# A fused Mamba and mixture-of-experts layer pair: shared-expert transposes between gate and up products, first expert tiles transposed early, two sets of spare rows

## The chip, the core and the metric

The kernel is one program on one core of a Trainium2 chip. The metric is the device time in microseconds (us), median of several executions. The engines are TensorE (PE, with its weight loads shown as PEld), VectorE (DVE), ScalarE (ACT), GpSimd (POOL) and SyncE (SP), which issues most DMAs. Each has its own in-order instruction stream; they meet by semaphores. TensorE writes into eight PSUM banks of 128 x 512 float32.

## The reference

Two residual blocks over x of 2 x 1024 tokens with 512 features, all in float32:

```python
x = x + attn(layernorm(x), ...)   # a Mamba block: in-projection, causal conv,
                                  # selective scan over 16 states, gate, out-projection
x = x + ffn(layernorm(x), ...)

def ffn(x):                       # T = 2048 tokens, H = 512
    h = rmsnorm(x) * norm_w ; flat = h.reshape(T, H)
    scores = softmax(flat @ router_w.T)            # E = 32 experts
    topk_w, topk_ids = top_k(scores, 4) ; topk_w /= topk_w.sum()
    routed = sum over the token's 4 experts of topk_w * (silu(g) * u) @ w2[e],
             with g, u = split(flat @ w1[e])       # 512 -> 2 x 256 -> 512
    shared = silu(flat @ sg) * (flat @ su) @ sd    # 512 -> 512 -> 512
    return x + routed + shared
```

Run on the given inputs, the reference's routing fills 79 tiles of 128 token slots, counted per expert and rounded up. The last expert has three of them.

## The kernel before

`front` (L109) holds everything up to the experts, `experts` (L1417 on) the routed part. Tokens stand in 16 tiles of 128.

**Mamba part.** Four segments of 512 tokens, 32 blocks `g` of (segment, 128 channels). It ends at about 1040 us. The change leaves its instructions alone, except on SP: after the first loads of the spread B and C rows, SP writes 128 zero rows behind `flat` (the normalised tokens in DRAM) and behind `out`, waits for both to land (`blank_stored`), and only then loads `w_out` and what follows in its queue.

**Shared part.** The order of TensorE's work is a written list, `closing_items()`. `ft(t)` transposes token tile t, `lg(t)` makes its router logits. Then, for each tile i, `gu(i)` is the gate product and the up product (8 matmul records each, of 128 x 512), into one pair of PSUM banks, `gu_ps[i % 2]`; `at(i)` transposes the activation (4 transposes), `dn(i)` is the down product (8 records), `rt(i)` the matmuls of the routing tables. The list runs `gu(i+1), at(i), dn(i), rt(i)`. ACT takes the silu of the gate (`silu_gate`, L775), copies the transposed activation from PSUM (`act_turned`, L780), and scales a residual row (`base_row`). DVE multiplies silu and up (`mult`, L957), adds the down product to the residual (`add`, L963), and between these computes the routing: `route_scores` ahead of `mult(0)`, `route_ids` behind it, `route_mask`, `route_counts`, `route_places`, `route_tables`, `route_hot` and `route_list` behind `add(0)` to `add(8)`. When the list of token slots is made, POOL gathers the rows of the first four expert tiles (`xg`, L1275). SP stores the finished residual rows to `out`.

**Expert part.** A barrier of all engines, then a loop over passes of four tiles, worked in pairs. `tiles` (L1445) skips passes that hold no tile, so 79 tiles make 20 passes and 80 tiles: the last one, tile 79, has only spare slots. For a pair TensorE makes `h` (L1613), transposes the rows of the next pair (`xT`, L1599), transposes the activation (L1624) and makes `y` (L1631). `rows_in` and `rows_out` for tiles 0 and 1 stand ahead of the loop. POOL gathers rows from `flat` (L1484) and scatters `y` into `out` with an add (L1499). Two tiles of one expert never hold the same token, so scatter j then need not wait for scatter j-1; otherwise `tile_wait[j]` makes it wait until that has landed. `same` in `route_counts` says which, and past the last expert it says "wait": every spare slot p of every tile points at the same row T + p.

## Time and profile before

| | us |
|---|---|
| median of 3 runs | 1807.21 |
| lowest, highest | 1803.53, 1816.69 |
| the profiled execution's own time | 1814.91 |
| its span, first to last instruction | 1813.2 |
| TensorE busy in the span | 1596.5 |
| mean granted TensorE clock | 0.963 of full |

The profiled execution lies 7.70 us above the median of the three. The Mamba part takes about 1040 us, where POOL and DVE are the fullest engines; the shared part runs from about 1075 to 1277 us, the expert part from there to the end, and in these two TensorE is the fullest.

### The profile page before, as it was taken

How to read it: one execution, taken by the hardware profiler on the slowest of the kernel's cores; microseconds unless marked ns; L12 is line 12 of the kernel's file. 1: busy time of each engine (PE TensorE's matmuls, PEld its weight loads, DVE VectorE, ACT ScalarE, POOL GpSimd, SP SyncE). 2: the span in 40 equal slices, each digit the busy share in tenths (PEclk: the TensorE clock that was granted, in tenths of full speed). 3: DMA queues.
4: the chain of work that ended last, by engine and by line, in shares of the span. 5: the costliest groups of instructions: out<-in, count | busy, mean ns of one | idle time of the engine just before them, and what ended most of it. 6: DMA issues, size and time to landing. Idle time of an engine off the chain costs nothing. (4 is left out here: it accounts for less than half of the span.)

```text
span 1813.2 us, 18146 instructions
## 1 busy us (share of the span) xinstructions
PE 1596.5 (88%) x4390; PEld 726.5 (40%) x4391; DVE 1187.3 (65%) x1675; ACT 736.4 (41%) x1231; POOL 1110.7 (61%) x704
## 2 busy tenths in 40 slices
PE   5678998899988999989887899999899999999995
PEld 2233433344433443333333364444444444444442
DVE  3599998999999989999999527531232323333331
ACT  4466566766566657666665421110011111111110
POOL 0199889998889998999999400010254454454442
PEclk9889998999999999999999999999999999999997
DMA  3620114101133111141000540010367686676653
GB/s 117 232 73 21 36 61 172 72 31 38 42 137 130 32 31 33 48 173 37 20 25 1 195 187 24 24 42 23 83 160 206 158 226 170 177 210 168 183 131 55
DMA packets 64838, 180.59 MB, mean 100 GB/s; under 512 B 10256, under 2 KB 15120, under 8 KB 56080
## 3 DMA queue, kind: packets, MB, share of 16 engines
q1 hardware_dynamic: 46704, 136.12, 21.3%
q0 software_dynamic: 18080, 43.82, 12.3%
q8 instruction: 25, 0.41, 0.1%
q14 instruction: 29, 0.24, 0.0%
HBM read 146.34 MB, written 33.57 MB: 99 GB/s over the span
## 5 line engine op out<-in xcount | busy, mean ns | idle before, releaser
L1217 POOL TENSOR_TENSOR h<-h,c_rep 128x2048 f32<-128x2048 f32 x128 | 579.4, 4530 | 34.7 <-DVE h L897 29.7
L1402 PE MATMUL bank<-h,ident 128*128 128x512 f32 x916 | 452.6, 638 | 95.6 <-POOL h L1217 74.7
L661 ACT ACTIVATE bank<-delta,a_neg 128x512 f32<-128x512 f32 x512 | 336.0, 682 | 183.2 <-DVE h L897 182.4
L1402 PEld LDWEIGHTS bank<-h,ident 128*128 128x128 f32 x916 | 181.1, 202 | 340.5 <-issue 211.9
L897 DVE TENSOR_TENSOR_SCAN h<-bank,state,h 128x512 f32<-128x512 f32 x256 | 305.9, 1260 | 0.2 <-ACT bank L661 0.2
L897 DVE TENSOR_TENSOR_SCAN h<-bank,h 128x512 f32<-128x512 f32 x256 | 290.7, 1200 | 2.0 <-ACT bank L661 2.0
L1613 PE MATMUL h_ps<-w_ring,xT 128*128 x640 | 284.8, 598 | 4.2 <-issue 4.2
L887 DVE TENSOR_TENSOR h<-bank,b_rep 128x2048 f32<-128x2048 f32 (+1 forms) x105 | 227.5, 2186 | 43.7 <-ACT bank L654 33.9
L1538 ACT ACTIVATE gs<-h_ps 128x256 f32<-128x256 f32 x80 | 30.7, 384 | 417.1 <-PE h_ps L1613 417.1
L1564 DVE TENSOR_TENSOR act<-gs,h_ps 128x256 f32<-128x256 f32 x80 | 33.7, 422 | 248.1 <-ACT gs L1538 248.1
L1613 PEld LDWEIGHTS h_ps<-w_ring,xT 128*128 128x128 f32 x640 | 120.7, 191 | 163.2 <-issue 163.2
L1631 PE MATMUL y_ps<-w_ring,aT 128*128 x320 | 148.7, 607 | 11.6 <-ACT aT L1542 11.5
L1483 POOL TENSOR_TENSOR held<-ones 128x1 f32<-128x1 f32 x78 | 22.2, 285 | 202.6 <-DVE which L1574 202.0
L1499 POOL DMA_INDIRECT out<-y,into x80 | 128.0, 1600 | 28.9 <-issue 26.4
L1204 POOL TENSOR_TENSOR h<-du,b_rep 128x2048 f32<-128x2048 f32 (+1 forms) x32 | 125.4, 3918 | 11.5 <-PE bank L1402 11.5
L1305 PE MATMUL bank<-xnT,w_in 128*128 128x512 f32 x256 | 118.5, 609 | 12.5 <-ACT zs L628 10.7
L1337 PE MATMUL bank<-xnT,w_res 128*128 128x512 f32 x256 | 120.3, 614 | 0.0
L1327 PE MATMUL bank<-w_out,xs 128*128 128x512 f32 x256 | 116.1, 597 | 0.0
L1484 POOL DMA_INDIRECT xg<-flat,which x78 | 79.3, 1016 | 22.6 <-POOL held L1483 12.0
L1498 POOL TENSOR_TENSOR sent<-ones 128x1 f32<-128x1 f32 x80 | 29.9, 373 | 97.7 <-DMA out<-y,into 85.8
L1631 PEld LDWEIGHTS y_ps<-w_ring,aT 128*128 128x128 f32 x320 | 57.8, 191 | 79.0 <-issue 79.0
L1274 POOL TENSOR_TENSOR held<-ones 128x1 f32<-128x1 f32 x4 | 0.8, 200 | 134.4 <-DVE which L1116 134.3
(213 smaller groups left out, 1746.4 us busy)
## 6 DMA issues: line engine op xcount, KB each, us to landing
w_ring<-in_w SPq DMA_DIRECT2D x32, 1024.0 KB, 6.0
b_rep<-bcd SPq DMA_DIRECT2D x16, 1024.0 KB, 6.8
c_rep<-bcd SPq DMA_DIRECT2D x16, 1024.0 KB, 4.8
w_ring<-in_w SPq DMA_DIRECT2D x32, 512.0 KB, 7.6
w_in<-in_w_in_x SPq DMA_DIRECT2D x32, 256.0 KB, 2.6
w_res<-in_w_in_res SPq DMA_DIRECT2D x32, 256.0 KB, 2.6
xa<-in_x SPq DMA_DIRECT2D x20, 256.0 KB, 3.0
xb<-in_x SPq DMA_DIRECT2D x16, 256.0 KB, 2.9
```

The costliest lines, as they stand in the source:

```text
L661: eng.activation(da[j][:], delta[:, g % 2], ACT.Exp, scale=a_neg[:, col:col + 1])\
L887: eng.tensor_tensor(h[:, q, a:b], du_ps[:].unsqueeze(1).to_broadcast([P, b - a, SEG]), b_rep[:, Q * q + a:Q * q + b, :], ALU.mult).then_in ...
L897: eng.tensor_tensor_scan(h[:, q, j, :], da[j][:], h[:, q, j, :], init, ALU.mult, ALU.add)\
L1204: eng.tensor_tensor(h[:, q, a:b], du[:].unsqueeze(1).to_broadcast([P, b - a, SEG]), b_rep[:, Q * q + a:Q * q + b, :], ALU.mult).then_inc(S ...
L1217: ins = eng.tensor_tensor(h[:, q], h[:, q], c_rep[:, Q * q:Q * q + Q, :], ALU.mult)
L1305: ins = eng.matmul(out[:], w_in[:, n % 2, k, :], xnT[:, s % 2, k, :], start=(k == 0), stop=(k == KC - 1))
L1327: eng.matmul(out[:], xs[:, s % 2, d, i * P:(i + 1) * P], w_out[:, d, :], start=(d == 0), stop=False)
L1337: ins = eng.matmul(out[:], w_res[:, i % 2, k, :], xnT[:, s % 2, k, :], start=(k == 0), stop=(k == KC - 1))
L1402: ins = eng.matmul(y_ps[:], c.ident[:], h[:, q, j, :], start=False, stop=(q == NQ - 1 and j == Q - 1))
L1499: eng.indirect_dma_start(out=dram.out_rows, out_offset=bass.IndirectOffsetOnAxis(ap=into[:, u:u + 1], axis=0), in_=y[:, u, :], in_offset=N ...
L1613: ins = eng.matmul(h_ps[i][:], xT[:, i, k, :], c.w1r[:, bass.ds(ring[i], 1), k, :].rearrange("p a n -> p (a n)"), start=(k == 0), stop=(k ...
L1631: ins = eng.matmul(y_ps[i][:], aT[:, i, k, :], c.w2r[:, bass.ds(ring[i], 1), k, :].rearrange("p a n -> p (a n)"), start=(k == 0), stop=(k ...
```

## The change

**Order.** `gu` is split into `gate` and `up`, with a semaphore each, and the list becomes `gate(i+1), at(i), up(i+1), dn(i), rt(i)`. `silu_gate` waits for the gate alone, `mult` for both.

**First expert tiles.** `xt(0)` and `xt(1)`, the transposes of the gathered rows of expert tiles 0 and 1, stand behind `at(15)` and ahead of `dn(15)`, into the banks of `gu_ps[0]`. DVE copies them to `xT` ahead of `add(15)`. `xT` now lies where `flat_T` of tiles 0 and 1 was. The expert part starts without them, its semaphores counted up to match.

**Spare rows.** A second set of 128 zero rows is written behind `flat` and `out`; spare slots of even tiles point at the first set, of odd tiles at the second (`trash`, from a fourth iota on POOL). `same` now is also 1 past the last expert. `wfull` goes; the weights are kept in `prob`. The list of slots is made with one instruction of another form (`miss`).

TensorE's order around shared tile 0, before (`w_sg` is the gate weight, `w_su` the up weight, `act_shared` the activation of tile i, `w_sd` the down weight; a wait stands in brackets):

```order
L1362 MATMUL bank<-w_sg,flat_T 128x512 [waits m_work_free0,f_shared_loaded]
L1362 MATMUL bank<-w_sg,flat_T 128x512 x3
L1362 MATMUL bank<-w_su,flat_T 128x512 x4
L1367 MATMUL bank<-ident,act_shared 128x128 [waits f_act_ready,m_work_free0]
L1367 MATMUL bank<-ident,act_shared 128x128 x3
L1372 MATMUL bank<-w_sd,act_shared_T 128x512 [waits m_work_free0,m_work_free1]
L1372 MATMUL bank<-w_sd,act_shared_T 128x512 x3
L1362 MATMUL bank<-w_sg,flat_T 128x512 [waits f_act_ready,m_work_free0,f_shared_loaded]
L1362 MATMUL bank<-w_sg,flat_T 128x512 x3
```

and in the change:

```order
L1372 MATMUL bank<-w_sg,flat_T 128x512 [waits m_work_free0,f_shared_loaded]
L1372 MATMUL bank<-w_sg,flat_T 128x512 x3
L1383 MATMUL bank<-ident,act_shared 128x128 [waits f_act_ready,m_work_free0]
L1383 MATMUL bank<-ident,act_shared 128x128 x3
L1372 MATMUL bank<-w_su,flat_T 128x512 [waits m_work_free0,f_shared_loaded]
L1372 MATMUL bank<-w_su,flat_T 128x512 x3
L1388 MATMUL bank<-w_sd,act_shared_T 128x512 [waits m_work_free0,m_work_free1]
L1388 MATMUL bank<-w_sd,act_shared_T 128x512 x3
L1372 MATMUL bank<-w_sg,flat_T 128x512 [waits f_act_ready,m_work_free0,f_shared_loaded]
L1372 MATMUL bank<-w_sg,flat_T 128x512 x3
```

The four transposes now stand between the gate and the up product, so that they are reached one product earlier, and the up product lies between them and the down product. On DVE nothing moves here: the `mult(0)` that gives `f_act_ready` still stands behind the whole of `route_scores`.

TensorE's order from shared tile 15's transposes into the expert part, before (`xg` are the gathered rows):

```order
L1367 MATMUL bank<-ident,act_shared 128x128 [waits f_act_ready,m_work_free0]
L1367 MATMUL bank<-ident,act_shared 128x128 x3
L1372 MATMUL bank<-w_sd,act_shared_T 128x512 [waits m_work_free0,m_work_free1]
L1372 MATMUL bank<-w_sd,act_shared_T 128x512 x3
L367 UNCONDITIONAL_BRANCH
L1589 UNCONDITIONAL_BRANCH [waits barrier_Pool_Activation_PE_DVE_SP_release]
L1599 MATMUL xT_ps<-ident,xg 128x128 [waits e_xT_ready,e_gathered0]
L1599 MATMUL xT_ps<-ident,xg 128x128 x3
L1599 MATMUL xT_ps<-ident,xg 128x128 [waits e_xT_ready,e_gathered1]
L1599 MATMUL xT_ps<-ident,xg 128x128 x3
L1447 UNCONDITIONAL_BRANCH
L1447 ISA
```

and in the change:

```order
L1383 MATMUL bank<-ident,act_shared 128x128 [waits f_act_ready,m_work_free0]
L1383 MATMUL bank<-ident,act_shared 128x128 x3
L1378 MATMUL bank<-ident,xg 128x128 [waits f_act_ready,e_gathered0]
L1378 MATMUL bank<-ident,xg 128x128 x3
L1378 MATMUL bank<-ident,xg 128x128 [waits f_act_ready,e_gathered1]
L1378 MATMUL bank<-ident,xg 128x128 x3
L1388 MATMUL bank<-w_sd,act_shared_T 128x512 [waits m_work_free0,m_work_free1]
L1388 MATMUL bank<-w_sd,act_shared_T 128x512 x3
L369 UNCONDITIONAL_BRANCH
L1603 UNCONDITIONAL_BRANCH [waits barrier_Pool_Activation_PE_DVE_SP_release]
L1463 UNCONDITIONAL_BRANCH
L1463 ISA
```

The eight transposes of `xg` moved from behind the barrier to ahead of the last down product. What follows the branch, the loads of the loop's registers and the first `h`, is unchanged.

The diff:

```diff
--- before.py
+++ after.py
@@ -160,4 +160,5 @@
         c.xg = over("xg", "xa", [P, PASS, ROW])
+        c.xT = over("xT", "b_rep", [P, 2, KC, P])
         c.which, c.held = new("which", [P, PASS], I32), new("held", [P, 1])
-        c.late = mem.home["b_rep"]
+        c.late = mem.home["b_rep"] + mem.size([P, 2, KC, P], F32)
         placed_at = [0]
@@ -183,4 +184,3 @@
         dest = inside("dest", [P, TT, TOPK])
-        wfull = inside("wfull", [P, TT, E])
-        trash, miss = inside("trash", [P, 1]), inside("miss", [P, NT])
+        trash_i, trash, miss = inside("trash_i", [P, NT], I32), inside("trash", [P, NT]), inside("miss", [P, NT])
         oh = inside("oh", [P, TOPK, TT, E])
@@ -233,5 +233,5 @@
         f_names = ("blank_made blank_stored shared_loaded stat mv_ready ln_chain rvar_ready ms_ready rrms_ready pool_chain "
-                   "scales_ready flat_ready base_made logits_done gu_done silu_done act_ready "
+                   "scales_ready flat_ready base_made logits_done gate_done up_done silu_done act_ready "
                    "iota_made chain max_ready exp_done mask_ready weights_ready counted tiles_ready tiles_turned hot_ready "
-                   "placed which_ready").split()
+                   "placed which_ready xt_done").split()
         F = {n: sem("f_" + n) for n in f_names}
@@ -314,3 +314,3 @@
         HALVED = ("out", "dtr", "bc")
-        UNBANKED = ("lg", "gu", "rt")
+        UNBANKED = ("lg", "gate", "up", "xt", "rt")
@@ -319,3 +319,4 @@
             last = lambda i, half: ("out", NSEG - 1, i, half)
-            ft, lg, gu = (lambda t: ("ft", 0, t, 0)), (lambda t: ("lg", 0, t, 0)), (lambda i: ("gu", 0, i, 0))
+            ft, lg, xt = (lambda t: ("ft", 0, t, 0)), (lambda t: ("lg", 0, t, 0)), (lambda u: ("xt", 0, u, 0))
+            gate, up = (lambda i: ("gate", 0, i, 0)), (lambda i: ("up", 0, i, 0))
             at, dn, rt = (lambda i: ("at", 0, i, 0)), (lambda i: ("dn", 0, i, 0)), (lambda i: ("rt", 0, i, 0))
@@ -326,5 +327,6 @@
             items += [lg(t) for t in range(8, 12)]
-            items += [gu(0), ft(12), ft(13), lg(12), ft(14), lg(13), ft(15), lg(14), lg(15)]
+            items += [gate(0), up(0), ft(12), ft(13), lg(12), ft(14), lg(13), ft(15), lg(14), lg(15)]
             for i in range(TT):
-                items += ([gu(i + 1)] if i + 1 < TT else []) + [at(i), dn(i), rt(i)]
+                items += [gate(i + 1), at(i), up(i + 1)] if i + 1 < TT else [at(i), xt(0), xt(1)]
+                items += [dn(i), rt(i)]
             return items
@@ -465,5 +467,6 @@
                 eng.wait_ge(F["blank_made"], 1)
-                eng.dma_start(dram.flat[T:T + P, :], blank[:]).then_inc(F["blank_stored"], 16)
-                eng.dma_start(dram.out[TT], blank[:, 0:DM]).then_inc(F["blank_stored"], 16)
-                eng.wait_ge(F["blank_stored"], 32)
+                for n in range(2):
+                    eng.dma_start(dram.flat[T + n * P:T + (n + 1) * P, :], blank[:]).then_inc(F["blank_stored"], 16)
+                    eng.dma_start(dram.out[TT + n], blank[:, 0:DM]).then_inc(F["blank_stored"], 16)
+                eng.wait_ge(F["blank_stored"], 64)
                 eng.dma_start(w_out[:], dram.w_out).then_inc(S["out_loaded"], 16)
@@ -557,3 +560,3 @@
                 eng.wait_ge(F["weights_ready"], 1)
-                eng.dma_start(dram.flat_w, wfull[:]).then_inc(c.weights_stored, 16)
+                eng.dma_start(dram.flat_w, prob[:]).then_inc(c.weights_stored, 16)
                 for i in range(3, TT):
@@ -775,3 +778,3 @@
                 def silu_gate(i):
-                    eng.wait_ge(F["gu_done"], i + 1)
+                    eng.wait_ge(F["gate_done"], i + 1)
                     after(eng, F["act_ready"], i - 1)
@@ -958,2 +961,3 @@
                     eng.wait_ge(F["silu_done"], i + 1)
+                    eng.wait_ge(F["up_done"], i + 1)
                     if i >= 2:
@@ -976,3 +980,3 @@
                     eng.tensor_tensor(prob[:], logits, row(mx[:], E), ALU.subtract).then_inc(F["max_ready"], 1)
-                    eng.wait_ge(F["iota_made"], 3)
+                    eng.wait_ge(F["iota_made"], 4)
                     for a, b in ((iota, iota_i), (iota_h, iota_i), (tok, tok_i), (thr, thr_i)):
@@ -1020,4 +1024,4 @@
                     ch.settle()
-                    eng.tensor_tensor(wfull[:], prob[:], mask[:], ALU.mult).then_inc(F["weights_ready"], 1)
-                    ch.add(eng.tensor_scalar(trash[:], tok[:, 0:1], float(T + 1), None, ALU.add))
+                    eng.tensor_tensor(prob[:], prob[:], mask[:], ALU.mult).then_inc(F["weights_ready"], 1)
+                    ch.add(eng.tensor_copy(trash[:], trash_i[:]))
                     ch.add(eng.tensor_scalar(tok1[:], tok[:], 1.0, None, ALU.add))
@@ -1040,3 +1044,3 @@
                     ch.add(eng.tensor_scalar(ecmp[:], end[:], tok[:, 0:1], None, ALU.is_lt))
-                    ch.add(eng.tensor_scalar(same[:], etile[:], float(E), None, ALU.is_lt))
+                    ch.add(eng.tensor_scalar(same[:], etile[:], float(E), None, ALU.is_ge))
                     ch.settle()
@@ -1046,3 +1050,3 @@
                     ch.settle()
-                    eng.tensor_tensor(same[:], same[:], eprev[:], ALU.mult).then_inc(F["tiles_ready"], 1)
+                    eng.tensor_tensor(same[:], same[:], eprev[:], ALU.max).then_inc(F["tiles_ready"], 1)
                     eng.tensor_scalar(etile[:], etile[:], float(E - 1), None, ALU.min).then_inc(F["tiles_ready"], 1)
@@ -1110,3 +1114,3 @@
                     slots = count_ps[:, LISTED:LISTED + NT]
-                    ch.add(eng.tensor_scalar(miss[:], slots, 0.0, trash[:], ALU.is_equal, ALU.mult))
+                    ch.add(eng.scalar_tensor_tensor(miss[:], slots, 0.0, trash[:], ALU.is_equal, ALU.mult))
                     ch.settle()
@@ -1155,2 +1159,7 @@
                         mult(i + 1)
+                    if i == TT - 1:
+                        for u in (0, 1):
+                            eng.wait_ge(F["xt_done"], u + 1)
+                            eng.tensor_tensor(c.xT[:, u], gu_ps[0][u][:].rearrange("p (k t) -> p k t", k=KC),
+                                              c.norm_f[:].unsqueeze(2).to_broadcast([P, KC, P]), ALU.mult)
                     add(i)
@@ -1264,2 +1273,3 @@
                 eng.iota(thr_i[:], pattern=[[P, NM]], base=0, channel_multiplier=0).then_inc(F["iota_made"], 1)
+                eng.iota(trash_i[:], pattern=[[0, NT // 2], [P, 2]], base=T + 1, channel_multiplier=1).then_inc(F["iota_made"], 1)
@@ -1355,3 +1365,3 @@
                             ins.then_inc(F["logits_done"], 1)
-                    elif kind == "gu":
+                    elif kind in ("gate", "up"):
                         eng.wait_ge(F["shared_loaded"], 16 * len(shared))
@@ -1359,6 +1369,12 @@
                         after(eng, F["act_ready"], i - 1)
-                        for w, to in ((w_g, gu_ps[i % 2][0]), (w_u, gu_ps[i % 2][1])):
-                            for k in range(KC):
-                                ins = eng.matmul(to[:], flT[:, i, k, :], w[:, k, :], start=(k == 0), stop=(k == KC - 1))
-                        ins.then_inc(F["gu_done"], 1)
+                        w, to, made = {"gate": (w_g, gu_ps[i % 2][0], "gate_done"), "up": (w_u, gu_ps[i % 2][1], "up_done")}[kind]
+                        for k in range(KC):
+                            ins = eng.matmul(to[:], flT[:, i, k, :], w[:, k, :], start=(k == 0), stop=(k == KC - 1))
+                        ins.then_inc(F[made], 1)
+                    elif kind == "xt":
+                        eng.wait_ge(c.gathered[i], 16)
+                        eng.wait_ge(F["act_ready"], TT - 1)
+                        for k in range(KC):
+                            ins = eng.transpose(gu_ps[0][i][:, k * P:(k + 1) * P], c.xg[:, i, k * P:(k + 1) * P], c.ident[:])
+                        ins.then_inc(F["xt_done"], 1)
                     elif kind == "at":
@@ -1431,3 +1447,3 @@
         sent = sb("sent", [P, 1])
-        xT = sb("xT", [P, 2, KC, P])
+        xT = c.xT
         gs = sb("gs", [P, 2, FI])
@@ -1549,3 +1565,3 @@
                 eng.sem_inc(S["y_ready"], 2)
-                eng.sem_inc(S["xT_ready"], 2)
+                eng.sem_inc(S["xT_ready"], 2 + 2)
                 eng.sem_inc(S["which_ready"], U)
@@ -1584,4 +1600,2 @@
-                for i in (0, 1):
-                    rows_out(i, i)
                 tiles(eng, pair)
@@ -1590,3 +1604,3 @@
             def _(eng):
-                eng.sem_inc(S["xT_done"], U)
+                eng.sem_inc(S["xT_done"], U + 2)
                 eng.sem_inc(S["aT_done"], 2)
@@ -1634,4 +1648,2 @@
-                for i in (0, 1):
-                    rows_in(i, 0, i, 0)
                 tiles(eng, pair)
@@ -1675,6 +1687,6 @@
     d.bcd = nc.dram_tensor("bcd", (NB * HALVES, 2 * NS, SEG), F32, kind="Internal").ap()
-    d.out = nc.dram_tensor("out", (TT + 1, P, DM), F32, kind="ExternalOutput").ap()
+    d.out = nc.dram_tensor("out", (TT + 2, P, DM), F32, kind="ExternalOutput").ap()
     d.out_rows = d.out.rearrange("t p n -> (t p) n")
     d.x1 = nc.dram_tensor("x1", (TT, P, DM), F32, kind="Internal").ap()
-    d.flat = nc.dram_tensor("flat", (T + P, ROW), F32, kind="Internal").ap()
+    d.flat = nc.dram_tensor("flat", (T + 2 * P, ROW), F32, kind="Internal").ap()
     d.flat_seg = d.flat[0:T, 0:DM].rearrange("(s t p) n -> s p t n", t=ST, p=P)
```

## Rows read from the trace of the kernel before

**Rows 1.** The page: the span.

```profile
span 1813.2 us, 18146 instructions
```

**Rows 2.** Stretches (from:to, length, busy by engine, clock, DMA share, GB/s), most of the shared part.

```profile
1100.00:1270.00 170.00, 158.39 (x465) 73.08 (x464) 65.98 (x235) 20.09 (x35) 4.96 (x8) 1.00 0.09 30
```

**Rows 3.** Timeline of PE (start, us, what, [idle before]), one shared tile without routing.

```profile
1142.79 3.60 PE L1362 MATMUL bank<-w_su,flat_T 128*128 128x512 f32 x8
1146.22 0.60 PE L1367 MATMUL bank<-ident,act_shared 128*128 128x128 f32 x4
1147.65 3.67 PE L1372 MATMUL bank<-w_sd,act_shared_T 128*128 128x512 f32 x8 [0.83 <-ACT act_shared_T L784]
1151.16 3.60 PE L1362 MATMUL bank<-w_sg,flat_T 128*128 128x512 f32 x8
```

**Rows 4.** Groups of PE by line and form, from 1097 to 1272 us.

```profile
L1372 PE MATMUL bank<-w_sd,act_shared_T 128*128 128x512 f32 x120 | 55.1, 601 | 12.4 <-ACT act_shared_T L784 12.4
```

**Rows 5.** Timeline of PE: four transposes, and the matmuls right behind them.

```profile
1065.74 0.63 PE L1346 MATMUL bank<-ident,flat_rows 128*128 128x128 f32 x4
1066.21 0.98 PE L1352 MATMUL bank<-w_router,flat_T 128*128 128x32 f32 x8
```

**Rows 6.** Timeline of PE and DVE around shared tile 0.

```profile
1089.50 3.68 PE L1362 MATMUL bank<-w_sg,flat_T 128*128 128x512 f32 x8
1093.02 3.60 PE L1362 MATMUL bank<-w_su,flat_T 128*128 128x512 f32 x8
1095.17 0.69 DVE L961 TENSOR_TENSOR act_shared<-gate_silu,bank 128x512 f32<-128x512 f32 x1
1101.39 3.60 PE L1362 MATMUL bank<-w_sg,flat_T 128*128 128x512 f32 x8
```

**Rows 7.** Timeline of PE: two idle stretches of the Mamba part, and eight matmuls behind each.

```profile
764.96 3.70 PE L1402 MATMUL bank<-h,ident 128*128 128x512 f32 x8 [2.73 <-POOL h L1217]
899.77 5.40 PE L1402 MATMUL bank<-h,ident 128*128 128x512 f32 x8 [2.87 <-POOL h L1217]
```

**Rows 8.** Timeline of DVE and PE: the mask of the routing, and the matmuls that wait for it.

```profile
1110.52 0.48 DVE L1016 MEMSET hit<- 128x512 f32 x1 [0.17 <-DVE cum L1014]
1113.19 1.02 PE L1376 MATMUL bank<-mask,tri 128*128 128x512 f32 x2
```

**Rows 9.** Timeline of PE: the end of the shared part, the first two pairs of experts.

```profile
1273.58 3.67 PE L1372 MATMUL bank<-w_sd,act_shared_T 128*128 128x512 f32 x8 [0.78 <-ACT act_shared_T L784]
1279.38 1.07 PE L1599 MATMUL xT_ps<-ident,xg 128*128 128x128 f32 x8 [2.13 <-DVEq L1550]
1282.59 8.82 PE L1613 MATMUL h_ps<-w_ring,xT 128*128 x16 [2.15 <-issue]
1296.60 7.03 PE L1613 MATMUL h_ps<-w_ring,xT 128*128 x16
```

**Rows 10.** The chain that ended last, its last scatters: start, us, what.

```profile
1792.99 4.81 DMA out<-y,into
1798.61 1.57 POOL out L1499
```

**Rows 11.** Timeline of POOL: two scatters without a wait; then their time to landing.

```profile
1706.54 1.62 POOL L1499 DMA_INDIRECT out<-y,into  x1 [0.50 <-issue]
1708.56 1.58 POOL L1499 DMA_INDIRECT out<-y,into  x1 [0.16 <-issue]
DMA to landing us min/median/max: 4.9/4.9/4.9
```

**Rows 12.** Waits, expert part: who, for whom, us in total, times, longest.

```profile
PE xT_ps L1599 <- DMA xg<-flat,which: 9.6, 11, 1.7
```

**Rows 13.** Timeline: an issue behind the zero rows, its use; the page: time to landing.

```profile
89.87 0.46 SPq L401 DMA_DIRECT2D xa<-in_x  x1
107.25 0.83 ACT L593 ACTIVATE xa<-xa,n_bias,n_scale 128x512 f32<-128x512 f32 x1
xa<-in_x SPq DMA_DIRECT2D x20, 256.0 KB, 3.0
```

## The prediction, before the change was timed

> **What bounds the kernel now.** I read the page first (the span, [rows 1]), then the busy times by stretch, then the timelines of TensorE and of whoever releases it. The change touches nothing in the Mamba part but two DMAs, so what matters is who sets the pace from 1075 us on. In the shared part TensorE is busy 158.39 of 170.00 us at clock 1.00 while DVE has 65.98 and ACT 20.09 [rows 2]: TensorE is the bound, and what can be won is its idle time. That idle time has one cause. In a shared tile the transposes start at 1146.22, the down product only at 1147.65, after 0.83 us of idling for ACT's copy of the transposed activation [rows 3]. Fifteen down products waited 12.4 us for it in all [rows 4]. In the expert part TensorE works through as well, with 9.6 us of waits for gathered rows in 11 places [rows 12]. The end is a chain of two scatters: the last one is issued at 1798.61, once the one before it has landed (1792.99 + 4.81) [rows 10].
>
> **The change, part by part.**
>
> *Tiles 1 to 14: a gain.* Each product of 8 records takes 3.43 us (1142.79 to 1146.22); transposes to down product take 1.43, the down product 3.51 because it starts from idle (1147.65 to 1151.16) [rows 3]. In the new order four transposes and the next matmuls lie 0.47 apart, as where no wait stands between (1065.74 to 1066.21) [rows 5]; the copy, over 1.43 us after the transposes began, hides under an up product of 3.43; and the down product takes 3.43. The tile falls from 4.94 to 3.90 behind its up product: 1.04 each, 14 × 1.04 = 14.6 us. Lower end: only the idle time itself goes, 14 × 0.83 = 11.6.
>
> *Tile 0: a new wait.* Today gate(1) starts at 1089.50 and the up product at 1093.02; the transposes follow at about 1096.4, one product later. In the change they are reached at 1093.02. But they need `mult(0)`, which DVE runs at 1095.17 for 0.69 us, behind all of `route_scores` [rows 6]. Neither the scores nor their order on DVE move. So TensorE idles from 1093.0 to 1095.9, 2.9 us, with everything queued behind it. Then come transposes, up(1) and dn(0): 1095.9 + 0.47 + 3.43 + 3.43 = 1103.2 for gate(2), which started at 1101.39 [rows 6]: 1.8 us later. To that comes the clock. Eight matmuls behind a wait of 2.73 us took 3.70, behind one of 2.87 us 5.40 [rows 7]. At 2.9 I take the second: 5.40 − 3.60 = 1.8 more. The sum is +3.6 us; the ends are +1.8, no clock loss, and +5.4, the loss taken twice.
>
> *Later waits on DVE.* `mult(i+1)` now must be done about one product after `add(i)` could start rather than three. The tightest place is the mask. It is complete at 1111.00 [rows 8], 9.6 us after dn(0) ended at 1101.39 [rows 6]. TensorE wanted it 11.8 us after that, at 1113.19 [rows 8]; now it wants it after 3.43 + 0.47 + 3.43 + 3.43 = 10.8. That leaves 1.2 us: nothing to pay, and if the slack fails the loss is a few tenths.
>
> *Tile 15 and the two early transposes: nothing.* The down product waits for ACT's copy in either order. Before, it started at 1273.58, 1.4 us after the transposes began [rows 9]; the eight new transposes take about 2 × 0.47 = 0.9 us and end within that time. DVE's two copies to `xT` run during the down product.
>
> *Start of the experts: a gain.* Before, eight transposes at 1279.38 take 1.07 us, then 2.15 us pass in the sequencer's register loads before `h` at 1282.59 [rows 9]. Those loads stand behind the transposes in the stream, so they now start 1.07 us earlier: −1.1. Ends: 0, if another engine's arrival at the barrier decides, and −2.2, if the wait was for `xT` and not for the loads. The clock loss there (8.82 for 16 records against 7.03 for the next pair [rows 9]) stays: the idle time is one piece of about 4 us instead of two of 2.1.
>
> *Last scatter: a gain.* Tile 79 holds only spare rows, so it no longer waits for tile 78. Two scatters without a wait stand 2.02 us apart, and landed 4.9 us after issue [rows 11]. So the last is issued at 1792.99 + 2.02 = 1795.0 instead of 1798.61: −3.6. Ends: −3.6, and −0.8 if two scatters in flight share one rate, so that the last lands 4.8 us after its neighbour; then only the pause between landing and issue (1797.80 to 1798.61) goes. I take −3.6, by the pair that was measured. The Trainium skill, "DMA: Bandwidth & Descriptors", section "Issuing engines are not separate DMA queues", says that all DMAs run on the same 16 engines and interleave; read strictly it gives the −0.8. The pair in the trace speaks against it.
>
> *The rest: nothing.* Two more writes of zero rows, some 256 KB each, delay SP. What it issues next and what is needed first is a tile of x, issued at 89.87 and used at 107.25; transfers of 256 KB land in 3.0 us [rows 13]. Two of them are 6 us against 17.4 − 3.0 = 14.4 us of cover; without it the start would slip one for one. The fourth iota on POOL, a wider copy and one changed instruction on DVE lie beside TensorE's products.
>
> **Sum:** +3.6 − 14.6 − 1.1 − 3.6 = −15.7 us. The profiled execution took 1814.91 us and would take 1799.2. The median of the three runs is 1807.21, 7.70 below the profiled one; nothing in the terms depends on that, so the forecast for the median is 1807.2 − 15.7 = **1791.5**.
>
> **Rivals.**
>
> *The clock holds at tile 0.* Then the stall costs 1.8 instead of 3.6, and with the upper end at the experts' start (−2.2) the time is 1791.5 − 1.8 − 1.1 = 1788.6. For it: 2.73 us of idling cost nothing [rows 7]. Against: 2.87 did.
>
> *The tail gives little.* The last scatter gains 0.8 or nothing, also if tile 79 were not a spare one and the new `same` changed nothing: 1794.3 to 1795.1. Against: it did wait, which a third tile of one expert would not.
>
> *The experts give it back.* Gathers queue on POOL behind scatters that wait, and TensorE waited 9.6 us for gathered rows [rows 12]. If the earlier start met worse transfers and doubled that: 1801.1. Against: POOL is fed by TensorE's results there, so both shift together.
>
> *Slower: the clock falls at every tile.* Between gate and up TensorE does nothing but four transposes. If that brought the half clock to the up product each time, it would take 3.43 us more, 15 × 3.43 = 51: 1791.5 + 51 = 1843. It decides from 15.7 / 15 = 1.05 us a tile. Against: the same four transposes, with 0.83 us of idling behind them, leave the clock at 1.00 over 170 us [rows 2]. The Trainium skill, "TensorE: Matmul & The Clock Gate", section "Part 4: PE-mode transpose", says that transposes do not count as TensorE being busy in the same way; by that rule this is the case to fear, and the row does not show it.
>
> **How the numbers follow.** Chances: forecast 0.55, clock holds 0.15, tail 0.12, experts 0.13, slower 0.05. The ends of all terms together give −2.2 − 3.6 − 14.6 + 1.8 = −18.6 and 0 − 0.8 − 11.6 + 5.4 = −7.0, and the three runs lie up to 9.5 us from their median, so a median of the change may lie some 4 us off. I give 1784 to 1801. That takes in every case but the last and the worst of the experts'. One per cent, 18 us, is about what a measurement of this kernel can tell from no change: the line is 1789.1. Below it lie most of "clock holds" and the low quarter of the forecast: faster 0.30. Slower only by the last rival: 0.04. Within 1%: 0.66.
>
> **What the new profile would show.** Right: no idle time ahead of the down products of tiles 1 to 14, a period of 10.8 us instead of 11.8; one wait of about 2.9 us for DVE's `act_shared` ahead of tile 0's transposes and a slow product behind it; the first `h` about 1 us closer to the end of the shared part; two last scatters 2 us apart. Wrong: waits for DVE ahead of later transposes or the mask's matmuls, a clock below 1.00 in the middle of the shared part, more than 9.6 us of waits for gathered rows, or a first scan block that starts later.

## The result, and the profile after

The changed kernel takes 1792.33 us (median of 5 runs, 1791.81 to 1795.08); before, five runs beside it have a median of 1810.09 (1803.53 to 1816.69). The ratio is 0.9895, with a 95% interval of 0.9876 to 0.9914: 1.05% faster, 17.8 us by the medians. Forecast were 1791.5 us and 15.7 us less. The profiled execution of the changed kernel took 1795.08 us, its span is the one to set against [rows 1]:

```profile
span 1793.4 us, 18167 instructions
```

So the two profiled spans differ by 19.8 us. I cut both traces at the same six events of TensorE and DVE, which gives seven stretches, and subtracted (all in us):

| from ... to | before | after | difference | forecast |
|---|---|---|---|---|
| start to gate(1) | 1089.50 | 1086.38 | −3.1 | 0 |
| gate(1) to gate(2), tile 0 | 11.89 | 13.84 | +1.95 | +3.6 |
| gate(2) to transposes of tile 15 | 170.81 | 155.90 | −14.9 | −14.6 |
| those to the end of its down product | 5.05 | 5.05 | 0 | 0 |
| end of that to the transposes behind the first pair of experts | 14.01 | 15.10 | +1.1 | −1.1 |
| from there to the result `y` of tile 78 | 499.41 | 498.12 | −1.3 | 0 |
| from there to the end | 22.5 | 19.0 | −3.5 | −3.6 |

First, most of the shared part, the stretch that answers to [rows 2] (from:to, length, busy by engine, clock, DMA share, GB/s):

```profile
1080.00:1251.00 171.00, 167.67 (x533) 81.08 (x532) 77.46 (x303) 24.41 (x41) 4.96 (x8) 1.00 0.09 30
```

TensorE was idle 11.6 us of 170 there; now it is 3.3 of 171, and 2.83 of those are one wait. The groups of TensorE from 1097 to 1257 us, against [rows 4] (line, operation, count | busy, mean ns | idle before):

```profile
L1388 PE MATMUL bank<-w_sd,act_shared_T 128*128 128x512 f32 x120 | 53.9, 592 | 0.0
L1372 PE MATMUL bank<-w_sg,flat_T 128*128 128x512 f32 x112 | 50.8, 596 | 0.0
L1372 PE MATMUL bank<-w_su,flat_T 128*128 128x512 f32 x112 | 50.4, 592 | 0.0
L1383 PE MATMUL bank<-ident,act_shared 128*128 128x128 f32 x60 | 9.0, 273 | 0.0
```

The 12.4 us of waits by fifteen down products are gone and no other group has taken them up. Busy time of a down matmul fell from 601 to 592 ns as well. The timeline of TensorE, two tiles, against [rows 3] and [rows 6] (start, us, what, [idle before]):

```profile
1086.38 3.68 PE L1372 MATMUL bank<-w_sg,flat_T 128*128 128x512 f32 x8
1092.88 0.63 PE L1383 MATMUL bank<-ident,act_shared 128*128 128x128 f32 x4 [2.83 <-DVE act_shared L965]
1093.35 3.60 PE L1372 MATMUL bank<-w_su,flat_T 128*128 128x512 f32 x8
1096.78 3.60 PE L1388 MATMUL bank<-w_sd,act_shared_T 128*128 128x512 f32 x8
1100.22 3.60 PE L1372 MATMUL bank<-w_sg,flat_T 128*128 128x512 f32 x8
1103.65 0.60 PE L1383 MATMUL bank<-ident,act_shared 128*128 128x128 f32 x4
1104.09 3.60 PE L1372 MATMUL bank<-w_su,flat_T 128*128 128x512 f32 x8
1107.52 3.60 PE L1388 MATMUL bank<-w_sd,act_shared_T 128*128 128x512 f32 x8
1110.95 1.02 PE L1392 MATMUL bank<-mask,tri 128*128 128x512 f32 x2
```

In tile 0 the predicted wait stands ahead of the transposes, 2.83 us long. But the up product behind it took 3.60 us, as anywhere: the clock did not fall. In tile 1 there is no gap at all, and the mask's matmuls, the place with 1.2 us of slack [rows 8], start without a wait: DVE has the mask ready at 1109.84, 1.1 us ahead of them. DVE's multiplication tells the two tiles apart:

```profile
1092.05 0.69 DVE L965 TENSOR_TENSOR act_shared<-gate_silu,bank 128x512 f32<-128x512 f32 x1
1097.08 0.69 DVE L965 TENSOR_TENSOR act_shared<-gate_silu,bank 128x512 f32<-128x512 f32 x1 [1.31 <-PE bank L1372]
```

For tile 0 DVE comes from the scores and TensorE waits for it. For tile 1 DVE has itself waited 1.31 us for TensorE's up product.

The end of the shared part, against [rows 9]:

```profile
1256.12 0.60 PE L1383 MATMUL bank<-ident,act_shared 128*128 128x128 f32 x4
1256.56 1.04 PE L1378 MATMUL bank<-ident,xg 128*128 128x128 f32 x8
1257.50 3.67 PE L1388 MATMUL bank<-w_sd,act_shared_T 128*128 128x512 f32 x8
1266.25 10.18 PE L1627 MATMUL h_ps<-w_ring,xT 128*128 x16 [5.08 <-issue]
1276.27 1.04 PE L1613 MATMUL xT_ps<-ident,xg 128*128 128x128 f32 x8
```

The eight early transposes (L1378) fit ahead of the down product at no cost. Yet the two idle pieces of 2.1 us and the transposes between them [rows 9] have become one idle piece of 5.08: `h` follows the end of the down product by 5.08 us, where it was 5.34. And the first pair of experts took 10.18 us instead of 8.82. The chain of waits (start, us, what) says what the 5.08 us are:

```profile
1262.80 0.08 issue
1262.90 3.35 issue
1266.25 10.18 PE h_ps L1627 x16
```

"issue" is time in which the engine waited for nothing that the profile shows, the sequencer being at work on instructions that do not count as busy. By the program's order these are, behind the barrier, the loads of the loop's registers: 3.35 us. That it is these loads and nothing else in the sequencer is read from the order; no run takes them out.

Last the tail, on POOL, against [rows 10]:

```profile
1776.71 1.57 POOL L1515 DMA_INDIRECT out<-y,into  x1 [0.48 <-issue]
1778.66 1.57 POOL L1515 DMA_INDIRECT out<-y,into  x1 [0.16 <-issue]
```

The last two scatters are issued 1.95 us apart, without a wait; before, tile 79's stood 5.62 us behind tile 78's (1792.99 to 1798.61). In the expert part TensorE's waits for gathered rows [rows 12] came to 6.0 us in 7 places.

Three lines of the table have no edit behind them: −3.1 ahead of gate(1), the size of the first pair of experts, and −1.3 in the loop of the experts. The experiments had to say what belongs to the change.

The clock stands behind the first two. Up to 980.5 us both traces run about 0.1 us or less apart. Then the same wait of TensorE, 3.44 us long in both, is followed by eight matmuls that took 5.40 us before (granted clock 0.68 from 987.68 to 993) and 3.70 us after (1.00):

```profile
987.68 5.40 PE L1402 MATMUL bank<-h,ident 128*128 128x512 f32 x8 [3.44 <-POOL h L1217]
```

```profile
987.64 3.70 PE L1418 MATMUL bank<-h,ident 128*128 128x512 f32 x8 [3.44 <-POOL h L1226]
```

By gate(0) the traces are 1.8 us apart (1075.21 and 1073.39), and gate(0) itself took 4.98 us before (clock 0.72 from 1075 to 1080) and 3.68 after: 1.3 more. So the 3.1 us are clock that one run lost and the other did not. The length of a wait alone does not decide it either: in the trace before, 2.35 us of idling were followed by 5.40 us for eight, and in the third trace of the change, told below, 3.08 us of idling by 3.70 us.

```profile
926.69 5.40 PE L1402 MATMUL bank<-h,ident 128*128 128x512 f32 x8 [2.35 <-POOL h L1217]
```

```profile
893.82 3.70 PE L1418 MATMUL bank<-h,ident 128*128 128x512 f32 x8 [3.08 <-POOL h L1226]
```

### The profile page after: what moved, and what is told of

It reads as the page before. It is cut to its first block and busy times, and to the rows that moved or that the text cites. A ratio compares the mean times of both kernels' runs of the same rounds, so it can differ in the third digit from the quotient of the medians.

```text
span 1793.4 us, 18167 instructions
## 1 busy us (share of the span) xinstructions
PE 1591.0 (89%) x4390; PEld 724.6 (40%) x4391; DVE 1186.4 (66%) x1675; ACT 737.5 (41%) x1231; POOL 1111.3 (62%) x705
## 3 DMA queue, kind: packets, MB, share of 16 engines
q0 software_dynamic: 18080, 43.82, 12.4%
## 5 line engine op out<-in xcount | busy, mean ns | idle before, releaser
L1315 PE MATMUL bank<-xnT,w_in 128*128 128x512 f32 x256 | 118.4, 609 | 12.6 <-ACT zs L631 10.8
L1315 PEld LDWEIGHTS bank<-xnT,w_in 128*128 128x128 f32 x256 | 48.8, 195 | 78.8 <-issue 58.0
```

Source lines behind the costliest of these rows:

```text
L1315: ins = eng.matmul(out[:], w_in[:, n % 2, k, :], xnT[:, s % 2, k, :], start=(k == 0), stop=(k == KC - 1))
```

## The experiments

All are edits of the changed kernel; the diffs show the lines that matter and leave out the bookkeeping that goes with them (storage, semaphore counts, sizes). "Before" ran beside them on the same chip in each of three sessions, with medians of 1813.77, 1813.85 and 1809.67 us. Totals of one kernel scatter by several us, so each experiment is read in two ways: its total, with the interval of the ratio to before, and its stages, from one trace each. In the shared part the stages repeat to 0.1 us; the start of the experts and the loop do not. The stages are: tile 0 (gate(1) to gate(2)), the period of a later shared tile, the start of the experts (end of the last down product to the transposes behind the first pair), and the loop (first `h` to `y` of tile 78).

My theory after the result: of what the change does, only the order of tiles 1 to 14 and the spare rows win time; the early transposes win nothing, because the register loads, not the transposes, end that wait; tile 0 costs the wait alone. The rival: the early transposes do win the microsecond that I forecast, and the clock took it back.

One thing stays in all the kernels of the next part: `silu_gate` waits for the gate product alone. It is worth 0.05 us a tile by itself. Before, ACT takes the SiLU of the next tile only when the up product is done, straight ahead of the copy that TensorE waits for, and TensorE waits 0.83 us; with the old order and the split semaphore it waits 0.78. From gate(1) to the transposes of tile 15 the two kernels with the old order below take 0.76 us less than the kernel before.

### One part at a time

**Only the order.** No early transposes, one set of spare rows with the old rule.

```diff
-                items += [gate(i + 1), at(i), up(i + 1)] if i + 1 < TT else [at(i), xt(0), xt(1)]
+                items += [gate(i + 1), at(i), up(i + 1)] if i + 1 < TT else [at(i)]
-            eng.tensor_scalar(same[:], etile[:], float(E), None, ALU.is_ge)
+            eng.tensor_scalar(same[:], etile[:], float(E), None, ALU.is_lt)
-            eng.tensor_tensor(same[:], same[:], eprev[:], ALU.max)
+            eng.tensor_tensor(same[:], same[:], eprev[:], ALU.mult)
```

> The kernel before with one part of the change: gate and up products split, the transposes of the tile before between them. No early expert transposes, one set of spare rows. Theory 1 (the order hides ACT's copy in tiles 1 to 14, 1.06 us each, and costs 1.9 us at tile 0): 14.9 - 1.9 = 13 us faster than before, at(15) reached 13 us earlier counted from gate(1); the two scatters at the end 5.6 us apart as before. Rival (part of the 17.8 us measured is not the change but the Mamba part's own run-to-run shift of some 3 us): the same 13 by stages, while the total may differ from it by 3. If the order is worth less than 10 us by stages, theory 1 is wrong.

Measured: 1802.3 us, ratio 0.9929 [0.9904, 0.9954], 11.5 us less than before. Tile 0 took 13.84 us (before 11.89), the later tiles' period 10.74 (before 11.80). The start of the experts took 15.45 and the loop 514.8. The wait at tile 0 is the same as in the full change:

```profile
1090.56 0.63 PE L1376 MATMUL bank<-ident,act_shared 128*128 128x128 f32 x4 [2.83 <-DVE act_shared L963]
1091.02 3.60 PE L1365 MATMUL bank<-w_su,flat_T 128*128 128x512 f32 x8
```

By its stages this part gives −14.9 + 1.95 = −13.0 us, of which 0.76 are the split semaphore, and again no slow product stands behind 2.83 us of idling.

**Only the early transposes.** The old order, one set of spare rows.

```diff
-                items += [gate(i + 1), at(i), up(i + 1)] if i + 1 < TT else [at(i), xt(0), xt(1)]
+                items += [gate(i + 1), up(i + 1), at(i)] if i + 1 < TT else [at(i), xt(0), xt(1)]
```

> The kernel before with only the transposes of expert tiles 0 and 1 moved ahead of the last down product. Theory 1 (the register loads of the loop ran beside the transposes already, so only 0.3 us goes, and the longer idle stretch costs clock at the first h, 8.8 to 10.2 us): 0 to 1 us slower than before by stages, no difference in the total. Rival (my forecast, the loads stood behind the transposes): 1.1 us faster, first h starting 4.2 us after the last down product ends. A third: the clock at the first h was luck of one profile: h takes 8.8 again and the total is 0.3 us faster.

Measured: 1812.71 us, ratio 0.9996 [0.9982, 1.0011]. The timeline of TensorE:

```profile
1265.79 1.04 PE L1377 MATMUL bank<-ident,xg 128*128 128x128 f32 x8
1266.73 3.67 PE L1387 MATMUL bank<-w_sd,act_shared_T 128*128 128x512 f32 x8
1275.48 9.39 PE L1626 MATMUL h_ps<-w_ring,xT 128*128 x16 [5.08 <-issue]
```

The transposes are out of the way and `h` still starts 5.08 us behind the down product. The interval reaches to 3.3 us of gain, so the total alone would not refute 1.1 us; the stage does. Over the profiled runs, the down product's end to `h` is 5.08 to 5.24 us where the transposes are early (eight traces without the filler that is told below), and 5.34, 5.34 and 5.49 where they are not: 0.1 to 0.4 us, not 1.07. Nor did the clock take anything back: from the first `h` to the transposes behind it there are 8.4 to 10.0 us in those eight traces and 8.7, 9.1 and 10.0 in the three others.

**Only the spare rows.**

```diff
-                items += [gate(i + 1), at(i), up(i + 1)] if i + 1 < TT else [at(i), xt(0), xt(1)]
+                items += [gate(i + 1), up(i + 1), at(i)] if i + 1 < TT else [at(i)]
```

> The kernel before with only the second set of spare rows and the new rule for tiles past the last expert. Theory 1: the last scatter is issued 2 us after the one before it instead of 5.6, the end comes 3.5 us earlier, nothing else moves: 3.5 us faster. Rival (two scatters in flight share one rate): 0.8 us faster. The two additional writes of zero rows: SP goes on 1.4 us later, no one waits.

Measured: 1809.61 us, ratio 0.9979 [0.9960, 0.9997], 4.2 us less than before by the medians. POOL's timeline at the end:

```profile
1791.44 0.18 POOL L1508 TENSOR_TENSOR sent<-ones 128x1 f32<-128x1 f32 x1 [7.84 <-DVE y L1592]
1792.10 1.57 POOL L1509 DMA_INDIRECT out<-y,into  x1 [0.48 <-issue]
1793.13 0.76 POOL L1508 TENSOR_TENSOR sent<-ones 128x1 f32<-128x1 f32 x1
1794.05 1.57 POOL L1509 DMA_INDIRECT out<-y,into  x1 [0.16 <-issue]
```

The instruction ahead of the last scatter (`sent`, L1508) runs while the scatter before it is still being issued: it waits for nothing. The pair stands 1.95 us apart, as in the full change. The last scatter follows `y` of tile 78 by 4.26 us here (1789.79 to 1794.05) and by 4.27 in the full change. With the old rule it was 7.94 (before), 7.41 (the kernel with the order alone) and 8.12 (the early transposes alone). That is 3.1 to 3.9 us, by how long tile 78's scatter takes to land; the forecast was 3.6. The end of the span follows the issue of the last scatter by 14.58 to 14.60 us in the three traces with the old rule and by 14.61 to 14.88 in the ten with the new one, so the scatter that is still under way costs the last one 0.3 us at most. Of the 4.2 us in the total, 0.76 belong to the split semaphore.

The gains of the three parts by their totals, 11.5, 1.1 and 4.2, add up to 16.8 us; as their intervals are 5 to 9 us wide, that is no proof, but it contradicts nothing above.

**The change again, twice**, to have it in the sessions of the runs that follow.

> The change itself once more, as the measure for the three kernels run with it on this chip: about 18 us faster than before. Its stages from the profile: 13.8 us from gate(1) to gate(2), 10.74 for a tile without routing, 5.1 us of idling ahead of the first h, last two scatters 2 us apart.

Measured: 1800.81 us, ratio 0.9916 [0.9890, 0.9943]. Tile 0 13.84, period 10.74, `h` 5.24 behind the down product: all as in the first trace. The loop, however, took 515.8 us, not 508.1, and the start of the experts 13.62, not 15.10.

> The change a third time, beside the next two. The first two gave 1792.3 and 1800.8 us, with stages alike to 0.3 us up to the experts' loop and 508 and 516 us from the first h to the last pair's y. The theory to test: that part swings with the waits for scatters and gathers. Expected between 1792 and 1801, and what it lies above 1792 stands in the loop.

Measured: 1795.63 us, ratio 0.9916 [0.9885, 0.9946]; the loop 511.0, the start of the experts 13.63. One kernel thus had medians of 1792.3, 1800.8 and 1795.6 us, and the shared part never moved by a tenth.

### Tile 0

**Tile 0 in the old order**, all else as in the change. Run in two sessions.

```diff
-                items += [gate(i + 1), at(i), up(i + 1)] if i + 1 < TT else [at(i), xt(0), xt(1)]
+                items += ([gate(i + 1), up(i + 1), at(i)] if i == 0 else [gate(i + 1), at(i), up(i + 1)]) if i + 1 < TT else [at(i), xt(0), xt(1)]
```

> The change, but tile 0 in the old order (gate(1), up(1), transposes of tile 0, down product). Theory 1 (tile 0's transposes wait 2.8 us for DVE's product behind the scores): that wait goes, ACT's 0.8 us comes back, 1.9 us faster than the change. Rival (the stall is harmless because DVE's later routing steps set the pace anyway): the same as the change, with a new wait of TensorE for the mask. With a clock loss behind the stall, which one profile did not show, 3.7 us faster.

Measured: 1794.87 us, ratio 0.9899 [0.9877, 0.9920]. Tile 0 took 11.84 us.

> The change with tile 0 in the old order, now beside the change on one chip. Theory: 2.0 us faster than the change by stages (gate(1) to gate(2) 11.84 instead of 13.84), which the swing of the experts' loop may hide in the total.

Measured: 1793.61 us, ratio 0.9897 [0.9873, 0.9922]; beside it the change had 1795.63. Tile 0 took 11.84 again. Both ways the new wait is worth 13.84 − 11.84 = 2.0 us by the stage, against a forecast of 1.8 for the wait and 1.8 for the clock. The two totals beside each other differ by as much, but their runs overlap (1788.40 to 1794.58 against 1790.96 to 1801.03).

**The cause of the wait.** DVE's `mult(0)` and ACT's SiLU of tile 0 moved ahead of the scores; the change's order kept.

```diff
+                silu_gate(0)
                 eng.wait_ge(F["max_ready"], 1)
                 eng.activation(prob[:], prob[:], ACT.Exp).then_inc(F["exp_done"], 1)
-                silu_gate(0)
...
+                mult(0)
                 route_scores()
-                mult(0)
```

> The change, with the silu and the product of tile 0 taken ahead of the router's scores on ACT and DVE. Theory (tile 0's transposes wait only for DVE's product, which stands behind the scores though its inputs are there 6 us earlier): the 2.8 us wait goes with nothing in its place, gate(1) to gate(2) takes 10.8 instead of 13.8, 3.0 us faster than the change. Rival (the routing on DVE is now the tighter chain, and one more table load of 1.28 us on ACT ahead of the exponential delays it): TensorE waits for the next product or for the mask instead, and the gain is under 1 us.

Measured: 1794.67 us, ratio 0.9887 [0.9862, 0.9912]; beside it the change had 1800.81. TensorE:

```profile
1087.27 3.68 PE L1372 MATMUL bank<-w_sg,flat_T 128*128 128x512 f32 x8
1090.78 0.60 PE L1383 MATMUL bank<-ident,act_shared 128*128 128x128 f32 x4
1091.22 3.60 PE L1372 MATMUL bank<-w_su,flat_T 128*128 128x512 f32 x8
1094.65 3.60 PE L1388 MATMUL bank<-w_sd,act_shared_T 128*128 128x512 f32 x8
1098.09 1.45 PE L1372 MATMUL bank<-w_sg,flat_T 128*128 128x512 f32 x3
```

The gap is gone; tile 0 takes 10.82 us, 3.0 less than in the change and 1.0 less than in the old order. The other 3 us of the difference in the totals are the loop (513.0 against 515.8 in the two traces). DVE did the multiplication at 1086.15, 1.1 us ahead of gate(1). So the wait came from the scores standing ahead of it on DVE, as the prediction said, and two instructions moved remove it. It costs nothing on DVE: the multiplication runs while DVE would wait for TensorE's logits, and the scores begin 0.20 us behind the start of gate(1) in either kernel. The rival's table load on ACT (1.28 us) runs at 1078.61, ten microseconds ahead of the exponential, and the mask's matmuls still start without a wait.

### The start of the experts

If TensorE is kept at work while it waits, does the clock hold, and what of the 5.1 us is left to wait for? **The filler**: 15 matmuls of an identity, 128 columns each, into a bank that is still free, between the barrier and the loop.

```diff
+                for n in range(15):
+                    eng.matmul(y_ps[0][:, 0:P], c.ident[:], c.ident[:], start=True, stop=True)
                 tiles(eng, pair)
```

> The change, with 15 matmuls of 128 x 128 by 128 columns (the identity by itself, some 3.2 us, their result overwritten unread) on TensorE between the barrier and the loop of the experts. Theory 1 (the register loads run beside TensorE's queue, and the clock falls in the 5.1 us of idling): the first h starts as late as before, 5.1 us after the last down product, but its pair takes 7.0 to 7.3 us instead of 9.2 to 10.0: 2.5 us faster than the change. Rival 1 (my forecast's premise: the loads start when the work ahead of them is done): the first h starts 3.2 us later, 1 to 3 us slower than the change. Rival 2 (the slow first pair is not the clock): h starts as late as before and is as slow, no difference.

Measured: 1799.37 us, ratio 0.9911 [0.9886, 0.9936]; beside it the change had 1800.81.

```profile
1263.26 3.59 PE L1651 MATMUL y_ps<-ident 128*128 128x128 f32 x30 [1.98 <-PEq L370]
1267.81 7.13 PE L1628 MATMUL h_ps<-w_ring,xT 128*128 x16 [0.96 <-issue]
1274.77 1.04 PE L1614 MATMUL xT_ps<-ident,xg 128*128 128x128 f32 x8
```

The filler (each matmul in two records) starts after 1.98 us and is busy for 3.59. Behind it only 0.96 us are left where 3.35 stood: what the sequencer does there, the register loads by the program's order, runs beside matmuls that are already queued. That explains why taking eight transposes out from ahead of it won next to nothing: it had been running beside the transposes all along. And the first pair of experts takes 7.13 us, nearly as the second pair before the change, 7.03 [rows 9]. From its start to the transposes behind it there are 6.96 us; in the eleven traces without a filler there are 8.4 to 10.0. The granted clock says the same (stretches: from:to, length, busy by engine, clock, DMA share, GB/s; the change, then with the filler):

```profile
1266.00:1276.00 10.00, 9.75 (x16) 4.21 (x17) 0.42 (x1) 0.39 (x1) 0.00 (x0) 0.68 0.01 2
```

```profile
1267.00:1275.00 8.00, 7.20 (x19) 3.33 (x20) 0.42 (x1) 0.41 (x2) 0.00 (x0) 1.00 0.00 0
```

So the 1.4 to 3.1 us above 6.96 are the clock, and they are there only with the idling ahead; what makes them 1.4 in one run and 3.1 in another is open. The filler is a little longer than what it fills: `h` starts 6.5 us behind the down product instead of 5.1 to 5.2. The start of the experts took 13.48 us, against 13.62 to 15.14 in the change and its variants without it: 0.1 to 1.7 us, less than the 2.5 expected, because `h` comes 1.3 us later.

**Filler and `mult(0)` together.**

> Both together: tile 0's product ahead of the scores, and the filling matmuls ahead of the experts. Theory: the two gains lie in different places and add up, 5.5 us faster than the change and 23 us faster than before. Rival (the experts' loop is held by its gathers and scatters and takes back what its start gains): 3 us faster than the change.

Measured: 1794.53 us (1787.5 to 1798.16), ratio 0.9882 [0.9854, 0.9910]. Tile 0 10.82, first pair of experts 6.97, start of the experts 13.51. By the stages this version is 3.0 + 0.1 to 1.6 us ahead of the change, not the 5.5 expected, again for the later `h`; by its total it cannot be told from the kernel with `mult(0)` alone (1794.67).

### The loop

The loop swung from 508.1 to 515.8 us with one and the same kernel, which is more than the whole tail. What does it hang on? Theory: the scatters. Where an expert begins, its first tile's scatter waits until that of the tile before has landed (`same` is 0 there), and gathers queue behind it on POOL. Rival: the bandwidth of the transfers themselves, whoever waits for whom. **No scatter waits**: `same` is always 1, so that only the wait for the scatter two tiles back is left, and each tile is scattered to a spare set. This leaves the experts' part out of the result; gathers, products and scatters are as many and as large, but the rows that are written are others.

```diff
-                    ch.add(eng.tensor_scalar(same[:], etile[:], float(E), None, ALU.is_ge))
+                    ch.add(eng.tensor_scalar(same[:], etile[:], 0.0, None, ALU.is_ge))
-                        eng.tensor_scalar(into[:, p + i:p + i + 1], c.slot_token[:, bass.ds(j, 1)], 0.0, None, ALU.add)
+                        eng.tensor_scalar(into[:, p + i:p + i + 1], c.trash[:, bass.ds(j, 1)], -1.0, None, ALU.add)
```

> The change, with every tile's rows added to the spare rows of its set, so that no scatter has to wait for the tile before it; it leaves out the routed part of the result. Theory (the experts' loop is held in places by scatters that wait for the one before, gathers queue behind them, TensorE waits 6 to 12 us for rows and loses clock behind some of these waits): the waits for gathered rows go to 0, TensorE's clock stays 1.00, the part from the first h to the last pair's y falls from 508 to 516 us to 490 to 493 us (40 pairs of 12.2 to 12.4), the total by 17 to 25 us, and the runs lie closer together. Rival (gathers and scatters are slow by themselves, whoever waits): the waits for rows stay above 4 us and the part above 500 us.

Measured: 1780.89 us (1777.58 to 1782.21), ratio 0.9837 [0.9819, 0.9854]; beside it the change had 1795.63. The loop took 492.7 us, as expected; the total fell by 14.7 us, short of the 17 to 25 expected. POOL's waits for a scatter to land fell from 83.7 us in 17 places (the change's second run) to 3.3 us in one. TensorE's groups in the loop, first in the change (its second run), then without the waits:

```profile
L1627 PE MATMUL h_ps<-w_ring,xT 128*128 x625 | 276.4, 595 | 2.3 <-issue 2.3
L1645 PE MATMUL y_ps<-w_ring,aT 128*128 x316 | 151.1, 622 | 11.4 <-ACT aT L1558 11.0
L1613 PE MATMUL xT_ps<-ident,xg 128*128 128x128 f32 x320 | 45.5, 281 | 10.9 <-DMA xg<-flat,which 10.8
```

```profile
L1628 PE MATMUL h_ps<-w_ring,xT 128*128 x624 | 276.0, 595 | 0.2
L1646 PE MATMUL y_ps<-w_ring,aT 128*128 x317 | 146.5, 605 | 11.3 <-ACT aT L1559 11.3
L1614 PE MATMUL xT_ps<-ident,xg 128*128 128x128 f32 x320 | 41.5, 273 | 0.0
```

Not one transpose waits for gathered rows any more: 10.8 us gone. The same transposes are 4.0 us shorter and the `y` products 4.6, which is the clock behind those waits. With the 2.1 us of issue that is 21.5 of the 23.1 us between the two loops. The first pair of experts belongs to the loop, and its slow clock has to do with the start and not with the scatters. Without it (first `h` to the transposes behind it) the loop is 498.1, 507.4 and 502.5 us in the change's three traces and 484.3 without the waits. In the change's first trace the waits for rows are 6.0 us, and transposes and `y` products are 3.9 us shorter than in its second: 8.7 of the 9.3 us between these two loops, of the same kind.

Is it the waits, or that writing to the spare rows is quicker? The scatters land no faster: their median is 7.0 us in the change's first trace, 7.5 in its second, 7.0 here. The bandwidth is no bound: the same bytes moved faster (stretches of the loop as above; the clock stands ahead of the DMA share and GB/s, the change's second run first, then without waits).

```profile
1275.00:1782.00 507.00, 482.39 (x1421) 231.93 (x1420) 163.92 (x475) 56.98 (x159) 235.93 (x312) 0.98 0.66 170
```

```profile
1273.00:1757.00 484.00, 472.50 (x1421) 227.92 (x1419) 161.03 (x477) 56.75 (x159) 236.53 (x312) 1.00 0.69 178
```

So the chain of scatters costs this loop 13.9, 23.2 and 18.3 us in the three traces, 60 to 75 per cent of it in waits and the rest in the clock behind them, and how much of it falls due in a run is what makes one kernel swing. What sets the landing of a scatter in a given run (4.3 to 8.7 us even here) stays open.

## Why the prediction was right, and where it was not

**Tiles 1 to 14, forecast −14.6: right.** Measured −14.9, 1.065 us a tile, in every trace with the new order. Of 1.04 forecast per tile 0.83 was idle time; the rest, the shorter transposes-to-next gap and the faster start of the down product, came too. Of the gain 0.05 us a tile comes with the split semaphore alone, which the forecast did not name.

**Tile 0, forecast +3.6: the step that failed is its clock term.** The wait was forecast as 2.9 us and is 2.83; its cost without the clock, forecast 1.8, is 1.95. The added 1.8 for a slow product did not come, in any of the six traces with that wait. Two rows stood for it, 2.73 us of idling without loss and 2.87 with [rows 7], and I took the nearer. That was a false reading: it took the length of the wait for what decides. In the same trace 2.35 us of idling were followed by eight matmuls of 5.40 us (926.69), and 3.44 us by 5.40 before and 3.70 after. At tile 0 the clock held six times out of six; why there, and not in the Mamba part, stays open. The rival "the clock holds at tile 0" had 0.15 and was the true one in that half, yet its own total also took −2.2 at the experts' start, which did not come.

**Later waits on DVE, forecast 0: right.** The mask's matmuls came up to it 10.73 us after gate(2) (1100.22 to 1110.95), forecast 10.8, and did not wait. No other wait for DVE appeared.

**Tile 15 and the early transposes, forecast 0: right**, 5.05 us from the transposes to the end in both.

**Start of the experts, forecast −1.1: wrong.** The step was "those loads stand behind the transposes in the stream, so they now start 1.07 us earlier". Order in the stream is not order in time there: the filler showed that the sequencer goes on while matmuls are queued. The traces give −0.1 to −0.4. The end 0 was in the forecast, but for another reason, an engine that comes late to the barrier. The other half of the step, "the clock loss there stays", held as to its being there and not as to its size: 1.4 to 3.1 us, from run to run, with and without the early transposes. In the pair of profiled runs it was 1.35 worse after, in the change's two later ones 0.2 to 0.3 better.

**Last scatter, forecast −3.6: right.** −3.5 in the full change, and the kernel with that part alone has the same spacing of 1.95 us and a total 4.2 us lower. The Trainium skill, "DMA: Bandwidth & Descriptors", section "Issuing engines are not separate DMA queues", taken strictly, would have given −0.8; the spacing of the issues, and an end that follows the last issue by 14.7 us instead of 14.6, speak for −3.5. So the rival "the tail gives little" (0.12) was not true.

**The rest, forecast 0: right.** SP goes on 1.3 to 1.4 us later (`w_out` at 89.10 instead of 87.66, x at 91.20 instead of 89.87), and nobody waits for it: x is used at 107.30 instead of 107.25. The 3.1 us ahead of gate(1) do not come from the change. They arise behind 980 us, from the clock. In the change's two other traces gate(1) starts at 1086.57 and 1084.75, and in the two kernels with the old order at 1083.41 and 1083.66, so this start moves by 5 us and more with the run.

**"The experts give it back" (0.13): not seen.** The waits for rows, 9.6 us before, came to 6.0, 10.8 and 10.7 us in the change's three traces, twice above the line that I had named as a sign of being wrong. But the kernels with the old order have loops of 508.1, 511.8 and 513.8 us, the change 508.1, 515.8 and 511.0: one swing, in which no loss to the change shows.

**The slower rival, clock falls at every tile (0.05), did not happen.** The granted clock is 1.00 over 171 us with four transposes between gate and up. By the rule of the Trainium skill, "TensorE: Matmul & The Clock Gate", section "Part 4: PE-mode transpose", transposes do not count as TensorE being busy in the same way; four of them in each tile do not show it here.

**The total.** It was closer than its parts. What the change itself does is −14.9 + 1.95 − 3.5 and some tenths for the experts: about −16.7 us, forecast −15.7. The two wrong terms cancel in part, tile 0 by −1.65 and the experts' start by about +0.8. On top lies what belongs to the runs: the three sessions gave −17.8, −13.0 and −14.0 us between medians, with intervals of 7 to 11 us for the difference. And the forecast started from the median of three runs before, 1807.21, where five gave 1810.09, so that the agreement of 1791.5 with 1792.33 to less than a microsecond is luck. With 1.05%, and an interval from 0.86 to 1.24%, the result lies at the line of 1% and cannot be put on either side of it; the forecast had given 0.30 and 0.66 to the two.

## What to carry to other kernels

Where an engine that bounds a stage idles for a copy of its own result, putting the next independent product in between wins the idle time and the slow restart in full, but look at the first tile: there the producer still has other work ahead, and moving that one small operation ahead in its stream is worth more than the order on the waiting engine (3.0 us against 2.0). Do not read a price for an idle stretch off two rows: look for every stretch of that length in the trace, and see whether they agree. Before taking an instruction out from ahead of "issue" time, ask whether the sequencer's work was running beside it already; a few dummy matmuls in that place tell. And read small changes by stages that the run does not disturb: those of the shared part repeated to 0.1 us while medians of the same kernel moved by 8.

## What the runs showed of the hardware

- **Idle time and clock.** In this kernel the length of an idle stretch of TensorE alone does not tell whether the clock falls. 2.83 us at tile 0 cost nothing in six traces; in the Mamba part 2.35 us were followed by eight matmuls of 5.40 us in all instead of 3.70, 3.08 us by eight that took 3.70, and 3.44 us at one and the same place by 5.40 us in one trace and 3.70 in another. 5.08 to 5.24 us cost 1.4 to 3.1 us on the next 16 matmuls, a size that changed from run to run; 3.59 us of dummy matmuls in between, with 1.98 and 0.96 us of idling around them, cost nothing.
- **The sequencer's own work**, register loads by the program's order, runs beside matmuls that are already queued: 3.35 us of it with an empty queue, 0.96 left behind 3.59 us of queued work.
- **Scatters that wait for each other** cost the expert loop 13.9 to 23.2 us of some 510, and the swing of one kernel between runs is of the same kind. Two scatters in flight at once, 1.95 us apart, cost 0.3 us at most.
